# Thirteen more down products formed from fp32r parts, low parts divided anew between VectorE and GpSimd, and all steps of the iterations placed anew

## Chip, core and metric

The kernel runs on one core of one Trainium2 chip. The metric is the device time of one execution in microseconds. TensorE multiplies matrices, VectorE (DVE in the rows), ScalarE (ACT) and GpSimd (POOL) work on elements, SyncE (SP) issues most transfers; each runs its own queue in order and meets the others by semaphores.

## The reference

Eight sequences of 512 tokens with 128 channels pass four residual blocks, each behind a layer norm:

```python
x = x + attention(layernorm(x))      # causal, one head of 128
x = x + moe(layernorm(x))            # router, 32 experts, top 4, swiglu(128 -> 64 -> 128), and a shared swiglu(128 -> 128 -> 128)
x = x + time_and_channel_mix(layernorm(x))   # two norms, token shift, recurrence over 512 tokens; relu^2 MLP 128 -> 512 -> 128
x = x + moe(layernorm(x))            # the same experts again
def swiglu(x, w1, w2, w3): return silu(x @ w1) * (x @ w3) @ w2
```

Everything is float32. The expert block is computed for all tokens by all experts, each hidden value weighted by its token's router weight, which is zero for experts not chosen.

## The kernel before

**Iterations and units.** The expert block of one sequence and one layer is an iteration `g`, 0 to 15 (0 to 7 the first layer, 8 to 15 the second). An iteration has 17 units: 16 pairs of experts (2 x 64 hidden values, 128 partitions) and the shared expert as unit 16. A unit `p` is: gate product `pa` (L1039, L1040, L1043), linear product `pb` (the same lines), `m_th` = silu or tanh of pa on ScalarE (L732, L734), `m_v` = m_th x pb on VectorE (L1468, or L1449 and L1471 after a tanh), `m_h` = m_v x router weight `m_wb` on GpSimd (L587), and the down product `py`, which sums over the units.

**Two forms of the down product.** The up products are all formed from parts: a value is split in a high part, rounded to fp32r, and a low part, the rest; high x high, low x high and high x low are three fp32r matmuls. The down product of a unit is either *native*, one fp32 matmul of m_h that the hardware runs as two passes (L1067), or formed from parts: ScalarE makes the high part `m_hh` (L921), VectorE or GpSimd the low part `m_hl` = m_h - m_hh (L416, `split_low`), then three fp32r matmuls (L1072 to L1074). The table `NATIVE` says which units of an iteration are native, `LOW_ON_POOL` whose low part is made by GpSimd, `LOW_LATE` which low parts stand behind VectorE's m_v of their slot instead of ahead of it, `TANH` which gates go by tanh: there VectorE computes (tanh + 1) x pa first (L1449), one VectorE step more, and no silu. The parts have `HALVES` = 3 buffers, m_h has `HIDDEN` = 5.

**The order.** Nothing is scheduled while it runs. Each engine's function `iteration` loops over slots, three for each unit; a unit's own steps have fixed slots, and each other step (attention of a coming sequence `att_step`, router of the next iteration `pro_step`, recurrence `time_begin` and `time_finish`, channel mix `channel_step`, and adding the result `add_out`) has a slot in a tuple written in the code, one number per sequence. So a number moves a step ahead of or behind units in its engine's queue. TensorE's matmuls of unit p wait for m_th and m_v of unit p - 2; its down product runs `LAG` = 4 units behind.

**Names used below.** `a_p`, `a_pT` (L1780): the two blends of the channel mix; `f_xl` (L1747): a low part of it; `t_ri` (L1785): a quarter of a reciprocal; `r_sel` (L1618), `r_ws` (L604), `r_w` (L1628): the router's selection, weights before and after the limit; L1231 and L1235: the matmuls that count the chosen tokens; `x_sb` (L669): GpSimd's addition to the residual.

Of the kernel before, what the change touches and what calls it, by code (L numbers as in the profile page):

```python
# [101 lines left out]
    (0, 2, 6, 7, 10, 14),
    (0, 1, 6, 8, 11, 13, 15),
    (1, 2, 3, 7, 9, 10, 12, 13, 14, 15),
    (0, 2, 7, 12),
# [60 lines left out]
def hybrid_kernel(nc, x_in, att_mats, mats, key_in, vecs, w_gate, w1_in, w3_in, w2_in, x_out):  # L166
    with ExitStack() as ctx:
# [377 lines left out]
        def _(pool):  # L545
# [48 lines left out]
            def pro_step(q, slot):
                if slot == (20, 10, 6, 7, 4, 4, 7, 11, 5, 1, 7, 7, 9, 4, 6, 0)[q]:
                    rsqrt(r_rs[:, :], r_ve[:, :], "r_vedone", q + 1, "r_rstd")
                if slot == (30, 32, 25, 30, 28, 32, 24, 35, 34, 31, 22, 37, 30, 37, 30, 22)[q]:
# [1304 lines left out]
```

## Time and profile before

| | us |
|---|---|
| median of three runs | 793.85 |
| lowest, highest | 793.61, 794.05 |
| span of the profiled execution | 791.7 |
| TensorE busy | 785.1 |
| VectorE, ScalarE, GpSimd busy | 645.9, 567.9, 625.3 |

The span runs from the first to the last instruction; some time before and behind it belongs to a run. The profile gives instructions with start and duration. Starts are measured; the ends of matmuls are modelled, so distances between starts tell what a matmul takes from the queue.

### The profile page before, as it was taken

What the parts mean: (1) busy time and instruction counts of PE and PEld (TensorE: products, weight loads), DVE (VectorE), ACT (ScalarE), POOL (GpSimd) and SP (SyncE); (2) the same over time, 40 slices, a digit from 0 to 9 for tenths busy, and PEclk for the clock granted to TensorE, in tenths of its full rate; (3) what the DMA queues carried; (4) which work ended last, traced back from release to release, by engine and by line L of the source; (5) the groups of instructions that cost most, each with busy time, mean ns of one, the idle gap of its engine ahead of it and who ended that gap; (6) DMA issues with size and microseconds to landing.
All of it is one profiled execution on the core that took longest, in us unless ns stands there. A gap on an engine that the chain in (4) does not pass through costs nothing.

```text
span 791.7 us, 12780 instructions
## 1 busy us (share of the span) xinstructions
PE 785.1 (99%) x3817; PEld 596.4 (75%) x3817; DVE 645.9 (82%) x1539; ACT 567.9 (72%) x1055; POOL 625.3 (79%) x491
## 2 busy tenths in 40 slices
PE   8999999999999999999999999999999999999998
PEld 5777778676776777768778777887778767788786
DVE  6875577997997989998988869988689889767686
ACT  5677787868768778689765867668685775677553
POOL 6687779849767797769987888998797877876985
PEclk9999999999999999999999999999999999999999
DMA  9353334243144342462425444253444424425552
GB/s 326 95 123 82 87 92 113 66 102 92 42 113 113 73 105 54 110 133 58 120 60 134 104 93 107 65 143 79 110 113 95 90 68 110 111 59 115 124 127 74
DMA packets 49332, 80.73 MB, mean 102 GB/s; under 512 B 3280, under 2 KB 14544, under 8 KB 48880
## 3 DMA queue, kind: packets, MB, share of 16 engines
q1 hardware_dynamic: 48976, 79.72, 42.1%
q8 instruction: 31, 0.51, 0.3%
q14 instruction: 37, 0.30, 0.1%
q10 hardware_dynamic: 288, 0.20, 0.1%
HBM read 75.19 MB, written 4.72 MB: 101 GB/s over the span
## 4 chain that ended last, share of the span: by engine, by line
PE 51%; POOL 2%; issue 2%; DVE 1%; ACT 0%; DVEq 0%; POOLq 0%; ACTq 0%
PE pa L1039 5%; PE pb L1039 4%; PE py L1067 4%; PE pa L1043 4%; PE pb L1043 4%; PE pa L1040 4%; PE pb L1040 4%; PE pu L1326 4%; PE py L1072 3%; PE py L1074 3%; PE py L1073 3%; POOL m_h L587 1%; PE pq L1283 1%; PE pu L1310 1%; PE pv L1334 1%
## 5 line engine op out<-in xcount | busy, mean ns | idle before, releaser
L587 POOL TENSOR_TENSOR m_h<-m_v,m_wb 128x512 f32<-128x512 f32 x254 | 364.3, 1444 | 98.7 <-DVE m_v L1468 42.9
L732 ACT ACTIVATE m_th<-pa 128x512 f32<-128x512 f32 x220 | 130.6, 594 | 102.0 <-PE pa L1043 97.7
L1468 DVE TENSOR_TENSOR m_v<-m_th,pb 128x512 f32<-128x512 f32 x205 | 138.6, 679 | 23.9 <-ACT m_th L732 15.5
L1039 PE MATMUL pa<-m_xh,w1h 128*128 128x512 f32 x272 | 137.2, 504 | 0.3 <-DVE m_v L1471 0.2
L416 DVE TENSOR_TENSOR m_hl<-m_h,m_hh 128x512 fp32r<-128x512 f32 x120 | 111.4, 929 | 24.8 <-ACT m_hh L921 24.1
L921 ACT ACTIVATE m_hh<-m_h 128x512 fp32r<-128x512 f32 x184 | 115.2, 626 | 13.8 <-POOL m_h L587 13.1
L1039 PE MATMUL pb<-m_xh,w3h 128*128 128x512 f32 x272 | 115.4, 424 | 0.0
L1043 PE MATMUL pa<-m_xl,w1h 128*128 128x512 f32 x272 | 107.3, 394 | 0.3 <-POOL m_xl L608 0.3
L1043 PE MATMUL pb<-m_xl,w3h 128*128 128x512 f32 x272 | 107.1, 394 | 0.0
L1040 PE MATMUL pa<-m_xh,w1l 128*128 128x512 f32 x272 | 106.6, 392 | 0.0
L1040 PE MATMUL pb<-m_xh,w3l 128*128 128x512 f32 x272 | 106.5, 391 | 0.0
L416 POOL TENSOR_TENSOR m_hl<-m_h,m_hh 128x512 fp32r<-128x512 f32 x64 | 86.1, 1345 | 12.6 <-ACT m_hh L921 12.1
L1072 PE MATMUL py<-m_hh,w2h 128*128 128x512 f32 x183 | 77.2, 422 | 0.0
L1074 PE MATMUL py<-m_hl,w2h 128*128 128x512 f32 x183 | 72.0, 394 | 0.0
L1073 PE MATMUL py<-m_hh,w2l 128*128 128x512 f32 x183 | 71.6, 392 | 0.0
L1039 PEld LDWEIGHTS pa<-m_xh,w1h 128*128 128x128 f32 x272 | 51.5, 189 | 25.5 <-issue 14.4
L1040 PEld LDWEIGHTS pa<-m_xh,w1l 128*128 128x128 f32 x272 | 51.5, 189 | 20.6 <-issue 14.6
L1039 PEld LDWEIGHTS pb<-m_xh,w3h 128*128 128x128 f32 x272 | 51.3, 189 | 14.0 <-issue 3.9
L1043 PEld LDWEIGHTS pa<-m_xl,w1h 128*128 128x128 f32 x272 | 51.1, 188 | 12.2 <-POOL m_xl L608 0.7
L1043 PEld LDWEIGHTS pb<-m_xl,w3h 128*128 128x128 f32 x272 | 51.1, 188 | 11.6
L1040 PEld LDWEIGHTS pb<-m_xh,w3l 128*128 128x128 f32 x272 | 51.4, 189 | 10.8 <-issue 1.9
L1449 DVE SCALAR_TENSOR_TENSOR m_th<-m_th,pa 128x512 f32<-128x512 f32 x52 | 35.2, 677 | 15.9 <-ACT m_th L734 15.8
(318 smaller groups left out, 1653.8 us busy)
## 6 DMA issues: line engine op xcount, KB each, us to landing
m_wb<-w_scratch SPq DMA_DIRECT2D x126, 512.0 KB, 6.5
x_sb<-in_x SPq DMA_DIRECT2D x8, 256.0 KB, 7.2
m_wb<-in_w SPq DMA_DIRECT2D x2, 1024.0 KB, 6.8
x_out<-x_sb SPq DMA_DIRECT2D x7, 256.0 KB, 6.6
u_scratch<-t_u SPq DMA_DIRECT2D x6, 256.0 KB, 2.6
t_u<-u_scratch SPq DMA_DIRECT2D x6, 256.0 KB, 2.7
f_kk<-in_w SPq DMA_DIRECT2D x1, 1024.0 KB, 9.7
w_scratch<-r_wT SPq DMA_DIRECT2D x16, 64.0 KB, 1.5
```

The source lines that it names most:

```text
L416: eng.tensor_tensor(m_hl[:, at, :], hidden(g, p), m_hh[:, at, :].bitcast(F32), ALU.subtract)\
L587: pool.tensor_tensor(hidden(g, p), gated(g, p), m_wb[:, p % (GRING * GP), :], ALU.mult).then_inc(sig["m_h"], 1)
L732: ins = act.activation(m_th[:, p % 2, :], pa[p % 2][:, :], ACT.Silu)
L921: act.activation(m_hh[:, halves_at(g, p), :], hidden(g, p), ACT.Copy).then_inc(sig["m_hh"], 1)
L1039: pe.matmul(ps[:, :], high[:, p, :], xh, start=True, stop=False)
L1040: pe.matmul(ps[:, :], low[:, p, :], xh, start=False, stop=False)
L1043: return pe.matmul(ps[:, :], high[:, p, :], xl, start=False, stop=True)
L1072: pe.matmul(py[:, :], w2h[:, p, :], hh, start=(p == 0), stop=False)
L1073: pe.matmul(py[:, :], w2l[:, p, :], hh, start=False, stop=False)
L1074: pe.matmul(py[:, :], w2h[:, p, :], hl, start=False, stop=(p == last_down(g))).then_inc(sig["m_y"], 1)
L1449: dve.scalar_tensor_tensor(out=m_th[:, r, :], in0=m_th[:, r, :], scalar=1.0, in1=pa[r][:, :], op0=ALU.add, op1=ALU.mult).then_inc(sig["m_u ...
L1468: dve.tensor_tensor(gated(g, p), m_th[:, r, :], pb[r][:, :], ALU.mult).then_inc(sig["m_v"], 1)
```

## The change

Thirteen units leave `NATIVE`: one in iterations 0, 1, 2, 4, 8 and 11, two in 3 and 6, three (1, 9, 11) in 7. Of their low parts VectorE makes eleven and GpSimd two; of the others, unit 14 of iterations 7 and 13, unit 16 of 14 and unit 3 of 15 go from GpSimd to VectorE, and unit 16 of iteration 2 the other way, so that VectorE makes 134 in place of 120 and GpSimd 63 in place of 64. 55 gates go by tanh in place of 52. Nearly all tuples of slots have new numbers, on all four engines; no step is added or dropped otherwise, and buffers, semaphores and fillers stay.

```diff
 NATIVE = (
-    (3, 9),
-    (11,),
-    (2, 3, 5, 6, 9, 10, 11, 12, 13),
-    (1, 2, 3, 4, 5, 7, 9, 10, 11, 12, 13, 14, 15),
-    (3, 5, 6, 7, 9, 10, 11, 13, 16),
+    (3,),
+    (),
+    (3, 5, 6, 9, 10, 11, 12, 13),
+    (1, 2, 3, 5, 7, 9, 10, 11, 12, 14, 15),
+    (3, 5, 6, 7, 10, 11, 13, 16),
     (1, 2, 7, 9, 10, 11, 12, 13),
-    (1, 3, 5, 7, 9, 15),
-    (1, 5, 7, 9, 11),
-    (1, 3, 5, 7, 9, 11, 16),
+    (3, 7, 9, 15),
+    (5, 7),
+    (1, 3, 5, 7, 11, 16),
...
 LOW_ON_POOL = (
...
-    (1, 2, 4, 8, 11, 12, 14),
-    (1, 3, 6, 8, 9, 10),
+    (2, 4, 8, 12),
+    (1, 3, 6, 8, 10),
...
             def channel_step(m, slot):
-                if slot == (40, 36, 38, 43, 41, 38, 44, 23)[m]:
+                if slot == (43, 45, 47, 46, 34, 37, 44, 22)[m]:
                     kept(pool, m)
                     pool.tensor_tensor(wide(chunk(m)), wide(chunk(m)), wide(t_u2[:, :, :]), ALU.add)\
                         .then_inc(sig["f_x"], 1)
```

**TensorE, iteration 7, around the linear product pb of unit 14.** Before, from the channel mix's product pu to the count of chosen tokens (L1231):

```order
L1310 MATMUL pu<-mt,a_pT 128x128 x4
L1039 MATMUL pb<-m_xh,w3h 128x512
L1040 MATMUL pb<-m_xh,w3l 128x512
L1043 MATMUL pb<-m_xl,w3h 128x512
L1334 MATMUL pv<-f_xh,key_h 128x512
L1335 MATMUL pv<-f_xh,key_l 128x512
L1336 MATMUL pv<-f_xl,key_h 128x512
L1231 MATMUL pq<-r_sel,tri_b 128x128
```

And now:

```order
L1310 MATMUL pu<-mt,a_pT 128x128 x4
L1231 MATMUL pq<-r_sel,tri_b 128x128
L1235 MATMUL pq<-r_sel,ones_b 128x128
L1235 MATMUL pq<-r_sel,ones_b 128x96
L1235 MATMUL pq<-r_sel,ones_b 128x64
L1235 MATMUL pq<-r_sel,ones_b 128x32
L1039 MATMUL pb<-m_xh,w3h 128x512
L1040 MATMUL pb<-m_xh,w3l 128x512
L1043 MATMUL pb<-m_xl,w3h 128x512
```

The count, which waits for r_sel, moved ahead of pb of unit 14; five matmuls stood between before.

**VectorE, the same place.** Before, from m_v of unit 11 to m_v of unit 13:

```order
L1468 TENSOR_TENSOR m_v<-m_th,pb 128x512
L1785 RECIPROCAL t_ri<-t_xr 128x128
L1780 SCALAR_TENSOR_TENSOR a_p<-a_g,vec,a_xT 128x512
L416 TENSOR_TENSOR m_hl<-m_h,m_hh 128x512
L1747 TENSOR_TENSOR f_xl<-a_p,f_xh 128x512
L1780 SCALAR_TENSOR_TENSOR a_pT<-a_g,vec,a_xT 128x512
L1468 TENSOR_TENSOR m_v<-m_th,pb 128x512
L1618 TENSOR_SCALAR r_sel<-r_rep 128x128
L1716 TENSOR_TENSOR t_n<-t_n,t_xv 128x512
L1468 TENSOR_TENSOR m_v<-m_th,pb 128x512
```

And now:

```order
L1468 TENSOR_TENSOR m_v<-m_th,pb 128x512
L416 TENSOR_TENSOR m_hl<-m_h,m_hh 128x512
L1785 RECIPROCAL t_ri<-t_xr 128x128
L1780 SCALAR_TENSOR_TENSOR a_p<-a_g,vec,a_xT 128x512
L1780 SCALAR_TENSOR_TENSOR a_pT<-a_g,vec,a_xT 128x512
L1747 TENSOR_TENSOR f_xl<-a_p,f_xh 128x512
L416 TENSOR_TENSOR m_hl<-m_h,m_hh 128x512
L1468 TENSOR_TENSOR m_v<-m_th,pb 128x512
L1618 TENSOR_SCALAR r_sel<-r_rep 128x128
L1468 TENSOR_TENSOR m_v<-m_th,pb 128x512
L416 TENSOR_TENSOR m_hl<-m_h,m_hh 128x512
L1716 TENSOR_TENSOR t_n<-t_n,t_xv 128x512
```

A second low part (that of unit 9) stands between m_v of unit 11 and of unit 12, and one more behind m_v of unit 13.

**GpSimd, the same place.** Before, from the channel mix's difference a_g on:

```order
L675 TENSOR_TENSOR a_g<-a_xT 128x512
L587 TENSOR_TENSOR m_h<-m_v,m_wb 128x512
L599 TENSOR_TENSOR r_p<-r_ex,r_ri 128x128
L587 TENSOR_TENSOR m_h<-m_v,m_wb 128x512
L669 TENSOR_TENSOR x_sb<-x_sb,t_u 128x512
L604 TENSOR_TENSOR r_ws<-r_sel,r_p 128x128
```

And now:

```order
L675 TENSOR_TENSOR a_g<-a_xT 128x512
L587 TENSOR_TENSOR m_h<-m_v,m_wb 128x512 x3
L599 TENSOR_TENSOR r_p<-r_ex,r_ri 128x128
L604 TENSOR_TENSOR r_ws<-r_sel,r_p 128x128
L587 TENSOR_TENSOR m_h<-m_v,m_wb 128x512
L416 TENSOR_TENSOR m_hl<-m_h,m_hh 128x512
```

The addition to x_sb left its place ahead of r_ws; it stands some units later.

## Rows read from the trace of the kernel before

**Rows 1.** The page: span, busy time of each engine, granted TensorE clock in forty slices.

```profile
span 791.7 us, 12780 instructions
PE 785.1 (99%) x3817; PEld 596.4 (75%) x3817; DVE 645.9 (82%) x1539; ACT 567.9 (72%) x1055; POOL 625.3 (79%) x491
PEclk9999999999999999999999999999999999999999
```

**Rows 2.** Busy time by stretches: start:end, length, each engine, clock, transfers.

```profile
0.00:24.20 24.20, 21.96 (x121) 14.21 (x121) 15.40 (x67) 13.65 (x34) 13.47 (x26) 1.00 0.89 291
24.20:373.70 349.50, 349.07 (x1695) 260.09 (x1694) 286.70 (x738) 269.17 (x504) 269.55 (x210) 1.00 0.39 91
373.70:419.50 45.80, 45.80 (x229) 35.86 (x228) 41.22 (x84) 31.84 (x57) 40.38 (x31) 1.00 0.45 106
419.50:748.80 329.30, 328.51 (x1606) 254.78 (x1605) 270.97 (x609) 231.83 (x425) 269.87 (x205) 1.00 0.43 100
748.80:791.70 42.90, 39.80 (x177) 31.47 (x176) 31.57 (x43) 21.38 (x38) 32.04 (x23) 1.00 0.40 99
```

**Rows 3.** Timeline of TensorE in iteration 7: start, duration, instruction.

```profile
402.60 0.39 PE L1072 MATMUL py<-m_hh,w2h 128*128 128x512 f32 x1
...
403.29 0.39 PE L1039 MATMUL pa<-m_xh,w1h 128*128 128x512 f32 x1
...
404.66 1.02 PE L1067 MATMUL py<-m_h,w2f 128*128 128x512 f32 x2
405.12 0.79 PE L1039 MATMUL pa<-m_xh,w1h 128*128 128x512 f32 x1
405.75 0.39 PE L1040 MATMUL pa<-m_xh,w1l 128*128 128x512 f32 x1
```

**Rows 4.** Groups and lines: count, busy and mean, or minimum/median/maximum ns.

```profile
L921 ACT ACTIVATE m_hh<-m_h 128x512 fp32r<-128x512 f32 x184 | 115.2, 626 | 13.8 <-POOL m_h L587 13.1
L416 DVE TENSOR_TENSOR m_hl<-m_h,m_hh 128x512 fp32r<-128x512 f32 x120 | 111.4, 929 | 24.8 <-ACT m_hh L921 24.1
L416 DVE TENSOR_TENSOR m_hl<-m_h,m_hh x120: 671/693/1792, 41.0 to 786.3; 128x512 fp32r<-128x512 f32 x120
L416 DVE TENSOR_TENSOR m_hl<-m_h,m_hh 128x512 fp32r<-128x512 f32 x6 | 6.9, 1150 | 0.0
L1449 DVE SCALAR_TENSOR_TENSOR m_th<-m_th,pa 128x512 f32<-128x512 f32 x52 | 35.2, 677 | 15.9 <-ACT m_th L734 15.8
L587 POOL TENSOR_TENSOR m_h<-m_v,m_wb x254: 1260/1300/2208, 38.9 to 784.4; 128x512 f32<-128x512 f32 x127
```

**Rows 5.** Timeline of VectorE in iteration 7, and TensorE's pb of unit 14.

```profile
401.30 0.68 DVE L1468 TENSOR_TENSOR m_v<-m_th,pb 128x512 f32<-128x512 f32 x1
...
402.75 1.68 DVE L1780 SCALAR_TENSOR_TENSOR a_p<-a_g,vec,a_xT 128x512 f32<-128x512 f32 x1
404.36 0.88 DVE L416 TENSOR_TENSOR m_hl<-m_h,m_hh 128x512 fp32r<-128x512 f32 x1
...
405.77 0.74 DVE L1780 SCALAR_TENSOR_TENSOR a_pT<-a_g,vec,a_xT 128x512 f32<-128x512 f32 x1
406.43 0.68 DVE L1468 TENSOR_TENSOR m_v<-m_th,pb 128x512 f32<-128x512 f32 x1
407.03 0.22 DVE L1618 TENSOR_SCALAR r_sel<-r_rep 128x128 bf16<-128x128 f32 x1
...
407.72 0.48 PE L1039 MATMUL pb<-m_xh,w3h 128*128 128x512 f32 x1
```

**Rows 6.** Timeline of GpSimd in the same stretch.

```profile
402.59 1.29 POOL L587 TENSOR_TENSOR m_h<-m_v,m_wb 128x512 f32<-128x512 f32 x1
...
407.24 1.76 POOL L587 TENSOR_TENSOR m_h<-m_v,m_wb 128x512 f32<-128x512 f32 x1 [2.55 <-issue]
408.97 1.29 POOL L669 TENSOR_TENSOR x_sb<-x_sb,t_u 128x512 f32<-128x512 f32 x1
```

**Rows 7.** Timeline of the end: the last instruction of TensorE.

```profile
788.21 0.38 PE L1394 MATMUL pu<-ident,m_y 128*128 128x128 f32 x2
```

More of the change, by code:

```diff
@@ L65 @@
 LOW_ON_POOL = (
-    (0, 2, 3, 7, 8, 9, 11, 12, 13, 14),
+    (0, 2, 3, 7, 8, 11, 12, 13, 14),
     (3, 4, 7, 10, 11, 13, 14, 15),
-    (2, 3, 6, 9, 10, 13, 14),
-    (3, 4, 6, 9, 10, 13),
-    (1, 7, 9, 14, 15),
+    (3, 6, 9, 10, 13, 14, 16),
+    (3, 6, 9, 10, 13),
+    (1, 7, 14, 15),
     (4, 5, 10, 12, 13, 14),
     (7, 11, 12),
-    (1, 2, 4, 8, 11, 12, 14),
-    (1, 3, 6, 8, 9, 10),
+    (2, 4, 8, 12),
+    (1, 3, 6, 8, 10),
     (0, 1, 3, 4, 6, 7, 11, 12, 14, 15),
@@ L78 @@
     (2, 5, 9, 12, 14, 15),
-    (4, 6, 7, 8, 10, 11, 14),
-    (12, 13, 14, 16),
-    (3, 9, 12, 16),
+    (4, 6, 7, 8, 10, 11),
+    (12, 13, 14),
+    (9, 12, 16),
 )
@@ L90 @@
 LOW_LATE = (
-    (0, 1, 3, 6, 7, 10, 13, 14, 15, 16),
+    (0, 1, 3, 6, 7, 9, 10, 13, 14, 15, 16),
     (0, 2, 4, 7, 9, 10, 16),
-    (1, 4, 7, 10, 12),
-    (1, 7, 11, 15),
-    (2, 4, 10, 12, 13),
+    (1, 2, 4, 7, 10, 12, 15),
+    (1, 4, 7, 11, 15),
+    (2, 4, 9, 10, 12, 13),
     (1, 8, 11, 16),
-    (2, 6, 8, 13, 15, 16),
-    (0, 1, 2, 3, 5, 6, 7, 8, 11, 12, 16),
-    (1, 7, 8, 12, 16),
+    (1, 2, 6, 8, 13, 15, 16),
+    (0, 1, 2, 3, 5, 6, 7, 8, 9, 11, 12, 14, 16),
+    (1, 7, 8, 9, 12, 16),
     (2, 10, 13, 15),
     (1, 2, 3, 5, 7, 10, 11),
[L102 to L105, printed above, removed]
+    (0, 2, 6, 7, 10, 14, 16),
+    (0, 1, 6, 11, 13, 15),
+    (1, 2, 3, 7, 9, 10, 12, 13, 15),
+    (0, 2, 6, 7, 12),
     (0, 1, 2, 5, 6, 7, 9, 10, 14, 16),
@@ L109 @@
 TANH = (
-    (0, 1, 6, 8, 11, 14),
+    (0, 1, 6, 8, 11, 14, 15),
     (15,),
@@ L114 @@
     (4, 6, 12, 13),
-    (12, 13),
+    (8, 12, 13),
     (12, 13, 15),
@@ L120 @@
     (2, 9, 13, 15),
-    (3, 9, 13, 15),
-    (1, 5, 11, 12, 16),
+    (3, 5, 9, 13, 15),
+    (5, 11, 12, 16),
     (3, 5, 8),
-    (),
-    (1, 2, 3, 4, 7, 9, 12),
+    (4, 9),
+    (1, 3, 4, 7, 9, 12),
 )
@@ L617, in weights_step @@
                     low_quarter(0, w3l, w3, w3h, 2)
-                if slot == (9,)[0]:
+                if slot == (6,)[0]:
                     low_quarter(1, w1l, w1, w1h, 1)
-                if slot == (24,)[0]:
+                if slot == (21,)[0]:
                     low_quarter(1, w3l, w3, w3h, 2)
-                if slot == (14,)[0]:
+                if slot == (8,)[0]:
                     low_quarter(2, w1l, w1, w1h, 1)
-                if slot == (23,)[0]:
+                if slot == (35,)[0]:
                     low_quarter(2, w3l, w3, w3h, 2)
-                if slot == (14,)[0]:
+                if slot == (11,)[0]:
                     low_quarter(3, w1l, w1, w1h, 1)
-                if slot == (35,)[0]:
+                if slot == (30,)[0]:
                     low_quarter(3, w3l, w3, w3h, 2)
-                if slot == (35,)[0]:
+                if slot == (37,)[0]:
                     low_quarter(0, w2l, w2_stage, w2h, 3)
-                if slot == (36,)[0]:
+                if slot == (39,)[0]:
                     low_quarter(1, w2l, w2_stage, w2h, 3)
@@ L1249, in spread_step @@
             def spread_step(slot):
-                if slot == (34,)[0]:
+                if slot == (38,)[0]:
                     pe.wait_ge(sig["r_wT"], 1)
@@ L1565, in pro_step @@
             def pro_step(q, slot, cmix):
-                if slot == (16,)[0] and q == 0:
+                if slot == (19,)[0] and q == 0:
                     dve.wait_ge(sig["a_add"], 2)
@@ L1787, in first_step @@
             def first_step(slot):
-                if slot == (27,)[0]:
+                if slot == (29,)[0]:
                     open_gate(0, 0)
                     gate(0, 0)
-                if slot == (35,)[0]:
+                if slot == (34,)[0]:
                     open_gate(0, 1)
                     gate(0, 1)
-                if slot == (35,)[0]:
+                if slot == (32,)[0]:
                     weigh(0)
-                if slot == (39,)[0]:
+                if slot == (38,)[0]:
                     weigh(1)
```

284 lines of the change are left out of this document (142 added, 142 removed), and 2 rows, old and new, of the table NATIVE.

## The prediction

> **What bounds the kernel now.** I read the busy line of the page first, then the busy time by stretches, then the instructions around one loaded place, and last the end. TensorE is busy 785.1 of 791.7 us, and its granted clock is full in all forty slices [rows 1]. So TensorE sets the time, and the question for every edit is whether it takes TensorE time away or makes TensorE wait. The stretches say where TensorE idles at all: 2.24 us before 24.2 us, 0.43 us in the first seven iterations, nothing in iteration 7, 0.79 us in iterations 8 to 14, and 3.1 us in the last one [rows 2]. That last part stands behind the last transpose (788.21 + 0.38), where VectorE adds and the output is stored [rows 7]; nothing in the change touches it. A busy TensorE can still hide short waits, since the ends of matmuls are modelled, but what idles openly inside the iterations is 0.43 + 0.79 = 1.2 us in all. Waits that the change removes can therefore bring little.
>
> The other engines have room, though not the same in every iteration. Over the span VectorE is busy 645.9, ScalarE 567.9, GpSimd 625.3 us [rows 1]. In iteration 7 VectorE is busy 41.22 of 45.80 us [rows 2], the tightest of those that the change loads most. Why this does not stop TensorE: TensorE works two units behind. At one place of iteration 7 VectorE's product m_v of unit 12 ends at 406.43 + 0.68 = 407.11, and the linear matmul that waits for it, pb of unit 14, starts at 407.72 [rows 5]: 0.6 us to spare, after five other steps had stood before it.
>
> **The change, part by part.**
>
> *Thirteen down products formed from parts.* Each removes one fp32 product (two passes, py<-m_h) and adds three fp32r products (py<-m_hh, m_hh, m_hl). The busy column misleads here, because a pass reads 590 ns and a fp32r product 390 ns while they overlap; the distance of starts counts. Three fp32r products start at 402.60 and the next unit's matmul at 403.29: 0.69 us. The fp32 product starts at 404.66; the record of the matmul after it begins early, inside the second pass, so I take the start of the one after that, 405.75, less one spacing of 0.23: 405.52, thus 0.86 us [rows 3]. Saved: 0.86 - 0.69 = 0.17 us a unit, 13 x 0.17 = 2.2 us, all on TensorE, which sets the end. No new matmuls elsewhere and the same fillers: TensorE's other work stays.
>
> *What they cost.* ScalarE makes 13 more high parts, 13 x 0.626 = 8.1 us on an engine that is busy 72% [rows 1, 4]: hidden. The low parts: VectorE makes 134 in place of 120, GpSimd 63 in place of 64. On VectorE one takes 929 ns in the mean, 671 at least, 693 in the median and 1792 at most [rows 4]. So 14 more cost 14 x 0.69 = 9.7 us if nothing blocks them, 13.0 us at the mean, 25.1 us at the worst row. Three more gates by tanh add three first steps, 3 x 0.68 = 2.0 us [rows 4]. VectorE goes from 646 to 658 to 661 us (83%); ACT_TABLE_LOADs stay at 62. Taken over the whole span this is hidden; by iterations it is not sure. Iteration 7 gets four of the fourteen (units 1, 9 and 11 newly formed, unit 14 taken from GpSimd). The six it has now take 6.9 us, 1150 ns each [rows 4]; at that price VectorE needs 41.2 + 4 x 1.15 = 45.8 us in an iteration that shrinks to 45.8 - 3 x 0.17 = 45.3. At 0.69 each it needs 44.0. What hides a low step is then gone to within -0.5 to +1.3 us, and VectorE also has waits of its own for TensorE that do not close up.
>
> *The steps placed anew.* The stretch of 929 over 693 ns is a low step that waits beside GpSimd: the scaling a_p starts at 402.75, takes 1.68 us where its sister a_pT takes 0.74, and GpSimd's m_h starts at 402.59 and runs 1.29 us [rows 5, 6]: VectorE stood until it ended. GpSimd pays too: m_h at 407.24 takes 1.76 against a median of 1.30 [rows 4, 6]. The Trainium skill ("SBUF — State Buffer", section Who interferes with whom) states it as a lock: a VectorE instruction with two SBUF inputs contends with a GpSimd instruction that reads SBUF, and the later one waits for the whole of the other. It speaks against this change, since each added low part has two SBUF inputs; the rows agree with it, and by it the fourteen could cost between 9.7 us and the 25.1 us of the worst row. Better placement gives VectorE and GpSimd time, and TensorE none unless it waits for them. I cost it at nothing, within bounds of -1.2 us (all open waits of the iterations go) and +1.6 us (somewhat more than as many come again).
>
> *One place by hand.* In iteration 7, from the start of m_v of unit 11 (401.30) to the end of r_sel (407.03 + 0.22 = 407.25), VectorE needs 5.95 us, with 0.94 us of blocking on a_p and 0.19 on the low step. After the change a second low step stands in this row (+0.69) and, if nothing blocks, 1.13 go: 5.5 us; if one step is blocked as a_p is now, 6.45 us. TensorE then asks for r_sel directly before pb of unit 14, so at 407.72 - 401.30 = 6.42 us behind the same point, 6.25 with the product of unit 9 shortened. So 0.7 us to spare or a wait of 0.2 us [rows 3, 5]. To the good, GpSimd's x_sb addition of 1.29 us (408.97) leaves its place before r_ws [rows 6]. I take 0.4 us of new waits in all, two such places, between 0 and 1.6.
>
> *The opening.* TensorE idles openly there for 2.24 us [rows 2]. On VectorE the shift a_sh and the conversion of w3 move behind one x_sb update, and on ScalarE r_ex moves ahead of two exponentials; the sum of the work before the router is the same. I cost this at nothing, within +-0.5 us.
>
> **Sum.** The profiled span is 791.7 us, the median of the three runs 793.85: 2.1 us lie around the span and stay. 791.7 - 2.2 + 0.4 = 789.9 us of span, so 792.0 us. A measurement of this kernel can tell about 0.2%, 1.6 us, from no change; the forecast of 1.8 us lies just past it.
>
> **The rivals.**
> 1. *Placement also removes waits.* With all of the product's saving and two thirds of the 1.2 us of open waits: 793.85 - 2.2 - 0.8 = 790.8 us. For it: nothing on TensorE stands against it. Against it: the waits of now are small and scattered, and VectorE gets 12 us more work.
> 2. *The saving is eaten by VectorE.* The price is the upper bound of new waits, 1.6 us, and somewhat more in iterations 3, 6 and 7, which take two or three new units each: 793.2 us, at most no change. For it: 0.6 us to spare at the place above. It is also the case that the new places do not avoid the blocking, so the change would not do what it says.
> 3. *Slower.* Iteration 7 becomes VectorE's. If its four new low steps are blocked as the worst row (1.79 us each), VectorE needs 41.2 + 7.2 = 48.4 us against 45.3: 3.1 us of wait, since pa and pb of each unit wait for m_v of two units before, and the backlog is carried into iteration 8. With one more iteration of this kind (6 or 3, half as much) it is 793.85 - 2.2 + 3.1 + 1.5 = 796.2 us. It begins to cost where the four steps take more than (45.3 - 41.2) / 4 = 1.0 us in the mean, and makes the kernel slower past 1.6 us in the mean. For it: 1.15 us is the mean there now. Against it: median 0.69, and a blocked step also ends blocks for the next.
>
> Less likely still is a long wait of ScalarE for the ring of three high and low parts, which now is passed by more units: iterations 13 and 14 hold 15 formed units of 17 already, as iteration 7 will, and lie in the stretch that loses 0.79 us in all [rows 2].
>
> **How the numbers follow.** Forecast (791.2 to 792.8): 0.45. Rival 1 (790.0 to 791.2): 0.18. Rival 2 (792.8 to 795.0): 0.21. Rival 3 (above 795): 0.16. The range 790.2 to 795.4 leaves out a little at the bottom and most of rival 3. Faster by over 0.2% means below 792.26: rival 1 and two thirds of the forecast, 0.50. Slower by over 0.2% means above 795.44: 0.15, nearly all of rival 3. The rest, 0.35, is the same.
>
> **What would show it.** Matmuls py<-m_hh 196 in place of 183, two-pass py<-m_h 26 fewer; TensorE busy lower by about 2 us and iteration 7 shorter by 0.5. Low parts on VectorE x134: a mean near 0.7 says that the placing works, 0.93 that it does nothing. TensorE's open idle in the stretches stays at 6.5 us in all. The forecast is wrong if starts of pa or pb wait for m_v in iterations 6 to 8, if VectorE shows no idle in iteration 7, or if the opening ends later than 24.2 us.

## The result and the profile after

| | median, us | lowest, highest | ratio to before, 95% interval |
|---|---|---|---|
| kernel before | 793.92 | 793.61, 794.05 | |
| changed kernel | 803.69 | 803.41, 804.33 | 1.0126 [1.0112, 1.0141] |

The change makes the kernel 9.8 us slower. The forecast was 792.0 us with a range up to 795.4: it has the wrong sign and its range does not hold the time.

The head of the page of the changed kernel, answering to [rows 1]:

```profile
span 802.0 us, 12854 instructions
PE 788.1 (98%) x3830; PEld 595.7 (74%) x3830; DVE 659.1 (82%) x1556; ACT 574.8 (72%) x1068; POOL 631.6 (79%) x490
PEclk9999999999999999999999999999999999999999
```

The clock is full, as before. VectorE's 659.1 us is what the prediction had (658 to 661). ScalarE has 6.9 us more than before, against the 8.1 reckoned for its high parts. GpSimd, for which the prediction gave no figure and which makes one low part less, is busier by 6.3 us. TensorE is not less busy by 2.2 us but busier by 3.0. Busy time by stretches, answering to [rows 2]; the third is iteration 7:

```profile
0.00:24.10 24.10, 21.39 (x121) 14.03 (x121) 15.40 (x67) 13.62 (x33) 13.48 (x26) 1.00 0.89 292
24.10:376.30 352.20, 350.48 (x1703) 259.99 (x1702) 297.55 (x745) 275.27 (x513) 279.06 (x214) 1.00 0.39 90
376.30:422.60 46.30, 45.65 (x232) 36.39 (x231) 41.46 (x87) 32.00 (x59) 40.82 (x29) 1.00 0.39 91
422.60:759.30 336.70, 331.07 (x1606) 253.81 (x1605) 273.25 (x615) 232.87 (x427) 270.06 (x204) 1.00 0.43 97
759.30:802.00 42.70, 39.54 (x177) 31.48 (x175) 31.44 (x44) 21.05 (x37) 28.23 (x20) 1.00 0.49 117
```

The opening and the last iteration with the end are no longer (24.1 and 42.7 us). The iterations between are 10.6 us longer: 2.7 in the first seven, 0.5 in iteration 7, 7.4 in the seven behind it, 3.1 of these in iteration 10 alone (from 49.7 to 52.8 us). TensorE's open idle is now 802.0 - 788.1 = 13.9 us, against 791.7 - 785.1 = 6.6.

Groups and lines, answering to [rows 3] and [rows 4] (count, busy, mean ns; idle before and what ended most of it):

```profile
L1072 PE MATMUL py<-m_hh,w2h 128*128 128x512 f32 x196 | 82.4, 420 | 0.4 <-POOL m_hl L416 0.4
L921 ACT ACTIVATE m_hh<-m_h 128x512 fp32r<-128x512 f32 x197 | 123.3, 626 | 21.1 <-POOL m_h L587 20.5
L416 DVE TENSOR_TENSOR m_hl<-m_h,m_hh 128x512 fp32r<-128x512 f32 x134 | 119.6, 894 | 22.0 <-ACT m_hh L921 21.4
L587 POOL TENSOR_TENSOR m_h<-m_v,m_wb 128x512 f32<-128x512 f32 x254 | 368.4, 1459 | 106.5 <-DMA m_wb<-w_scratch 42.7
```

The counts are those of the change. A low part on VectorE takes 894 ns in the mean: it was 929, and 0.7 us was the mark for "the placing works". GpSimd now waits 42.7 us in all for the transfer that brings the router weights, m_wb; in the same group of the kernel before, most of the idle time was for VectorE:

```profile
L587 POOL TENSOR_TENSOR m_h<-m_v,m_wb 128x512 f32<-128x512 f32 x254 | 364.3, 1444 | 98.7 <-DVE m_v L1468 42.9
```

For the transfer it waited 12.3 us there, in 5 places. What TensorE waits for, after (total us, times, longest):

```profile
PE pa L1039 <- DVE m_v L1471: 2.3, 4, 0.9
...
PE pq L1231 <- ACT t_r L855: 1.5, 2, 0.8
...
```

Before, that view has nothing above 0.3 us but the 1.6 us of the opening:

```profile
PE pq L977 <- POOL minus_half L551: 1.6, 1, 1.6
PE pv L1218 <- ACT m_xh L808: 0.3, 1, 0.3
```

There is no one new bottleneck: beside the same 1.6 us of the opening the view lists many waits of 0.2 to 0.9 us, for VectorE, ScalarE and GpSimd alike.

**How large the waits are in all.** The saving of the products is real. TensorE in iteration 7 of the changed kernel:

```profile
402.87 1.02 PE L1067 MATMUL py<-m_h,w2f 128*128 128x512 f32 x2
...
403.96 0.39 PE L1040 MATMUL pa<-m_xh,w1l 128*128 128x512 f32 x1
...
405.10 0.39 PE L1072 MATMUL py<-m_hh,w2h 128*128 128x512 f32 x1
...
405.79 0.39 PE L1039 MATMUL pa<-m_xh,w1h 128*128 128x512 f32 x1
```

403.96 - 402.87 - 0.23 = 0.86 us for the two passes, 405.79 - 405.10 = 0.69 us for the three fp32r products, as in [rows 3]. Wherever in this kernel a gate product pa stands right behind the down product, the distances are the same: 0.86 us in the median of 26 native products, 0.69 in that of 158 from parts. Without any new wait a kernel with the 13 parts would have a span of 791.7 - 2.2 = 789.5 us. The changed kernel has 802.0: 12.5 us of new waits. Of these 7.3 show as idle (13.9 - 6.6); the other 5.2 are counted as busy (788.1 - 785.1 + 2.2). Below, "new waits" is always the span less 789.5 (kernels with the parts) or less 791.7 (without them).

### The profile page after: what moved, and what is told of

It is laid out like the page before. It is cut to its first block and busy times, and to the rows that moved or that the text cites. A ratio compares the mean times of both kernels' runs of the same rounds, so it can differ in the third digit from the quotient of the medians.

```text
span 802.0 us, 12854 instructions
## 1 busy us (share of the span) xinstructions
PE 788.1 (98%) x3830; PEld 595.7 (74%) x3830; DVE 659.1 (82%) x1556; ACT 574.8 (72%) x1068; POOL 631.6 (79%) x490
## 5 line engine op out<-in xcount | busy, mean ns | idle before, releaser
L587 POOL TENSOR_TENSOR m_h<-m_v,m_wb 128x512 f32<-128x512 f32 x254 | 368.4, 1459 | 106.5 <-DMA m_wb<-w_scratch 42.7
L732 ACT ACTIVATE m_th<-pa 128x512 f32<-128x512 f32 x217 | 128.8, 594 | 102.5 <-PE pa L1043 95.6
L921 ACT ACTIVATE m_hh<-m_h 128x512 fp32r<-128x512 f32 x197 | 123.3, 626 | 21.1 <-POOL m_h L587 20.5
L416 DVE TENSOR_TENSOR m_hl<-m_h,m_hh 128x512 fp32r<-128x512 f32 x134 | 119.6, 894 | 22.0 <-ACT m_hh L921 21.4
L1039 PE MATMUL pa<-m_xh,w1h 128*128 128x512 f32 x272 | 132.2, 486 | 3.2 <-DVE m_v L1471 2.3
L1039 PE MATMUL pb<-m_xh,w3h 128*128 128x512 f32 x272 | 117.4, 432 | 0.7 <-DVE m_v L1468 0.5
L1072 PE MATMUL py<-m_hh,w2h 128*128 128x512 f32 x196 | 82.4, 420 | 0.4 <-POOL m_hl L416 0.4
L1074 PE MATMUL py<-m_hl,w2h 128*128 128x512 f32 x196 | 77.1, 393 | 0.0
L1073 PE MATMUL py<-m_hh,w2l 128*128 128x512 f32 x196 | 76.7, 391 | 0.0
L1072 PEld LDWEIGHTS py<-m_hh,w2h 128*128 128x128 f32 x196 | 36.9, 188 | 12.0 <-issue 3.3
```

The costliest lines, as they stand in the source:

```text
L416: eng.tensor_tensor(m_hl[:, at, :], hidden(g, p), m_hh[:, at, :].bitcast(F32), ALU.subtract)\
L587: pool.tensor_tensor(hidden(g, p), gated(g, p), m_wb[:, p % (GRING * GP), :], ALU.mult).then_inc(sig["m_h"], 1)
L732: ins = act.activation(m_th[:, p % 2, :], pa[p % 2][:, :], ACT.Silu)
L921: act.activation(m_hh[:, halves_at(g, p), :], hidden(g, p), ACT.Copy).then_inc(sig["m_hh"], 1)
L1039: pe.matmul(ps[:, :], high[:, p, :], xh, start=True, stop=False)
L1072: pe.matmul(py[:, :], w2h[:, p, :], hh, start=(p == 0), stop=False)
```

## The experiments

All times are medians; the kernel before took 792.7 to 793.9 us beside them, so times of runs that did not stand beside each other compare to about 1 us, and better by their ratios. Spans and waits are those of the one profiled execution.

**1. The parts alone, the places alone.** e1 is the kernel before with the `NATIVE` of the changed kernel and the low parts of just these 13 units as there; e2 is the kernel before with all slots of the changed kernel and its own four tables.

```diff
 # e1_parts_only: only the tables
 NATIVE = (
-    (3, 9),
-    (11,),
+    (3,),
+    (),
...
 # e2_places_only: only the slots
-                if slot == (40, 36, 38, 43, 41, 38, 44, 23)[m]:
+                if slot == (43, 45, 47, 46, 34, 37, 44, 22)[m]:
...
```

> The kernel before with only the thirteen units of the change formed from parts: NATIVE as after, the low parts of these units on the engine and in the half slot that the change gives them, every other step where it stood before. Theory P (the new places of the steps cost the time, the parts save it): TensorE saves 2.2 us and waits little more, 791.5 to 793.0 us. Theory V (VectorE's added low parts cost it): eleven more low parts of 0.9 us stand in unchanged queues and the worst of it shows here, 799 us or more.

> The slots of all steps as after, the four tables (NATIVE, LOW_ON_POOL, LOW_LATE, TANH) as before. Theory P: without the parts' saving of 2.2 us but with the waits, 803 to 806 us. Theory V: 793 to 795 us.

Measured: e1 803.6 us, ratio 1.0129 [1.0114, 1.0145], span 801.8; e2 803.7 us, 1.0134 [1.0119, 1.0150], span 802.0. Each half alone costs what both cost together: 12.3 us of new waits for the parts at the old places, 10.3 for the new places without the parts, 12.5 for both. So the new places do hold the parts better (they bring 12.3 us of waits at the old places and 2.2 more at the new, just what their products save), but are themselves 10 us worse. Two causes had to be looked for.

**2. Why the parts cost 12 us: take the added work away, piece by piece.** In e1, e6 makes the 13 added low parts for 64 of 512 tokens, e9 the high parts too; e14 makes no added low part at all (a memset of one column, 59 ns on VectorE and 99 on GpSimd, keeps its waits and its signal), e15 is e14 with short high parts.

```diff
 # e6, e9 (low parts)
+            n = 64 if (g, p) in ADDED else S
-            eng.tensor_tensor(m_hl[:, at, :], hidden(g, p), m_hh[:, at, :].bitcast(F32), ALU.subtract)\
+            eng.tensor_tensor(m_hl[:, at, 0:n], hidden(g, p)[:, 0:n], m_hh[:, at, 0:n].bitcast(F32), ALU.subtract)\
 # e9, e15 (high parts)
-                act.activation(m_hh[:, halves_at(g, p), :], hidden(g, p), ACT.Copy).then_inc(sig["m_hh"], 1)
+                n = 64 if (g, p) in ADDED else S
+                act.activation(m_hh[:, halves_at(g, p), 0:n], hidden(g, p)[:, 0:n], ACT.Copy).then_inc(sig["m_hh"], 1)
 # e14, e15 (low parts)
+            if (g, p) in ADDED:
+                eng.memset(m_hl[:, at, 0:1].bitcast(F32), 0.0).then_inc(sig[signal], 1)
+                return
```

> e1_parts_only, with the low parts of the thirteen added units computed for 64 of their 512 tokens only (the rest of their buffers keeps what stood there), so that each takes some 0.2 us in place of 0.7 to 1.8 of VectorE or GpSimd; ScalarE's high parts and TensorE's three products stay. Theory V (in the old places the time of the low step delays m_v and what stands behind it): the waits of 12 us go and the saving of 2.2 us remains, 791.5 to 794.5 us. If ScalarE's added high parts or the ring of three buffers is what TensorE waits for: 800 us or more.

> The kernel e6_low_short with, besides the low parts, the high parts of the 13 added units too made for 64 of 512 tokens only (that part of the output is not computed). TensorE still has 773.2 us of own work, against 775.4 in the kernel before; every step stands in its queue with its waits, only the 13 added steps of ScalarE are about 0.5 us shorter each. e6_low_short took 798.5 us, with 7.3 us more TensorE waits than the kernel before. Theory: the rest of these waits is ScalarE's added time, 0.63 us each, which makes m_th, the copies for the router and the norm late for TensorE. Then most of it goes and the time is 791.5 to 793.5 us. Rival: it is the place in the queue and not the time: ScalarE stands at an added high part until GpSimd's m_h is there, and what is behind it starts late however short the step is. Then the time stays at 797 to 799 us. In between, both count, in that share.

> The kernel e1_parts_only in which the 13 added low parts are not made: in place of each stands a memset of one column with the same wait and signal, so that what these products add is not computed; their fp32r matmuls and high parts stay. In e6_low_short the 11 steps on VectorE for 64 tokens still took 643 ns in the mean (one 1.30 us beside GpSimd's m_h), against 218 at least and 937 for the whole ones, so that experiment took away only a third of VectorE's added time. Theory: the waits come from the time that the low steps hold VectorE and GpSimd, standing beside each other's instructions included. From e1_parts_only to e6_low_short the time fell by 5.1 us for about 5.2 us less work on both; the remaining 7.7 us would bring all of the rest, down to 791.5 to 794 us, about the kernel before less the 2.2 us of the products. Rival: what costs is that ScalarE stands at an added high part for GpSimd's m_h, and that a product now needs two steps more before it, m_hh and m_hl, however short: then it stays at 796.5 to 799 us.

> The same as e14_no_low, and the 13 added high parts for 64 of 512 tokens only: nearly all added work of the three engines is gone, and only the waits at the added places are left. By the first theory 791 to 792.5 us, at most 1 us under e14_no_low; by the rival still 796 us or more.

| | median | ratio to before, interval | span | new waits | new waits by the median |
|---|---|---|---|---|---|
| e1, all work | 803.6 | 1.0129 [1.0114, 1.0145] | 801.8 | 12.3 | 12.3 |
| e6, low short | 798.5 | 1.0068 [1.0053, 1.0083] | 796.7 | 7.2 | 7.2 |
| e9, low and high short | 798.6 | 1.0068 [1.0051, 1.0085] | 795.0 | 5.5 | 7.3 |
| e14, no low | 795.0 | 1.0020 [1.0011, 1.0030] | 793.8 | 4.3 | 3.7 |
| e15, no low, high short | 793.4 | 1.0002 [0.9993, 1.0011] | 791.6 | 2.1 | 2.1 |

The last column takes the median less 1.8 us (what lies around the span) in place of the profiled span. It matters for e9, whose profiled execution was the fastest of its four (796.7): short high parts brought nothing on top of short low parts.

The low steps are 8.6 of the 10.3 us that e1 lies above before (803.6 - 795.0), the high steps 1.6 (795.0 - 793.4). 2.1 us of waits remain with hardly any work left, and take back the product's whole saving. So of 2.2 us saved nothing is left even where the added work is nearly free.

Where they stand can be read from e15: no down product of TensorE shows a wait there. Its longest wait that the kernel before does not have is for a copy of ScalarE, r_p, in the stretch of iteration 3, which takes 1.2 us more than before. ScalarE, then TensorE, in e15:

```profile
188.71 0.26 ACT L927 ACTIVATE m_hh<-m_h 128x64 fp32r<-128x64 f32 x1 [1.88 <-POOL m_h L592]
...
194.66 0.33 PE L1230 MATMUL pq<-ident,r_p 128*128 128x128 f32 x1 [0.80 <-ACT r_p L817]
```

And the same place of ScalarE before:

```profile
186.75 1.64 ACT L904 ACTIVATE a_xn<-x_sb,a_sh,a_q 128x128 f32<-128x128 f32 x4
```

An added high part of 0.26 us makes ScalarE stand 1.88 us for GpSimd's m_h. The step behind it, a_xn, started at 186.75 before and starts at 188.87 now, and r_p behind that at 194.34 in place of 192.68. So it is the place of the high part in ScalarE's queue, not its length. Of the remaining 0.9 us 0.4 stand in iteration 11, where TensorE waits 0.5 us for another copy of ScalarE, t_k; the rest is not followed.

From e6 and e9 alone one would read that ScalarE's time is no cause and only its place in the queue is. e14 and e15 show that both are. The groups of e6 show why short low steps were no clean test; the first row is VectorE's, and under it stand GpSimd and VectorE in iteration 8 at one of the added units:

```profile
L418 DVE TENSOR_TENSOR m_hl<-m_h,m_hh 128x64 fp32r<-128x64 f32 x11 | 7.1, 643 | 1.8 <-ACT m_hh L923 1.8
```

```profile
455.72 1.29 POOL L589 TENSOR_TENSOR m_h<-m_v,m_wb 128x512 f32<-128x512 f32 x1
455.79 1.30 DVE L418 TENSOR_TENSOR m_hl<-m_h,m_hh 128x64 fp32r<-128x64 f32 x1
```

A step for an eighth of the tokens, 218 ns at the least, takes 643 in the mean and here 1.30 us: it ends at 457.09, 0.08 us behind GpSimd's m_h beside it. Against the 937 ns of the group in e1 shortening had removed only a third of VectorE's added time. e14, which puts a step without SBUF inputs in its place, was the test.

How one such step becomes a wait of TensorE shows in e1, iteration 8 (all engines, in order of start):

```profile
459.72 1.29 POOL L587 TENSOR_TENSOR m_h<-m_v,m_wb 128x512 f32<-128x512 f32 x1
459.77 1.79 DVE L416 TENSOR_TENSOR m_hl<-m_h,m_hh 128x512 fp32r<-128x512 f32 x1
...
464.38 1.80 DVE L1671 SCALAR_TENSOR_TENSOR t_ea<-t_pp,decay 128x512 f32<-128x512 f32 x1
...
466.21 1.06 ACT L859 ACTIVATE t_ea<-t_ea 128x1024 f32<-128x1024 f32 x1 [2.34 <-DVE t_ea L1671]
...
467.18 0.61 ACT L921 ACTIVATE m_hh<-m_h 128x512 fp32r<-128x512 f32 x1
...
467.87 1.26 POOL L416 TENSOR_TENSOR m_hl<-m_h,m_hh 128x512 fp32r<-128x512 f32 x1 [2.24 <-ACT m_hh L921]
...
469.28 0.47 PE L1072 MATMUL py<-m_hh,w2h 128*128 128x512 f32 x1 [1.23 <-POOL m_hl L416]
```

The added low part (459.77) is blocked beside m_h; VectorE's step t_ea of the recurrence comes late and is blocked in its turn; ScalarE stands 2.34 us for t_ea, and behind that exponential stands the high part of another unit; GpSimd stands 2.24 us for it, and TensorE 1.23 us for the low part. In the kernel before, no low step stands at this place; t_ea takes 0.90 us there, and the same down product, formed from parts before too, does not wait. So here the price is paid through VectorE, ScalarE and GpSimd by steps behind the edit, not by the new step's own product.

The parts have three buffers, and a fourth might seem a remedy. The traces give it nothing to remove: neither in e1 nor in the changed kernel does a high part wait for TensorE to give a buffer back; the only waits listed for m_hh (19.9 and 20.5 us) are for GpSimd's m_h.

**3. Why the new places cost 10 us: the late router.** In the changed kernel TensorE's transpose of the weights (L1246, slot in L1239) and ScalarE's copy r_wT (L823, slot in L816) stand later for many iterations. e4 makes only this change to the kernel before; e3 and e5 undo it in the changed kernel, e3 for the weights of all iterations but 8 and 14, e5 for those of iterations 3 to 7, 9, 12, 13 and 15. In some of them both also move VectorE's r_w and TensorE's count to their earlier slots.

```diff
 # e4_router_end_late (kernel before)
-                if slot == (37, 43, 41, 43, 43, 43, 42, 43, 43, 43, 44, 44, 44, 47, 42, 39)[q]:
+                if slot == (38, 43, 41, 44, 46, 44, 44, 45, 48, 46, 44, 44, 45, 52, 44, 43)[q]:
...
-                if slot == (31, 44, 41, 44, 42, 44, 42, 44, 45, 47, 45, 46, 44, 47, 46, 39)[q]:
+                if slot == (31, 44, 41, 45, 45, 44, 42, 44, 48, 47, 45, 47, 45, 48, 47, 45)[q]:
```

> The kernel after, with the last steps of the router (the count's matmuls L1226 ff, VectorE's r_w, the transpose of r_w, ScalarE's copy r_wT that the transfer of the weights waits for) at the earlier of their two slots, before's or after's, in all iterations but 8 and 14. Theory R (the weights of the next iteration land late, GpSimd waits for them 42.7 us in place of 12.3, and TensorE with it): 796 to 800 us, and GpSimd's wait for the landing near 15 us. If the landing is not what TensorE waits for: 802 to 805 us.

> The kernel before, with only the transpose of r_w on TensorE and the copy r_wT on ScalarE at the later of their two slots, before's or after's. Theory R: GpSimd's wait for the landing rises from 12 to about 40 us and the kernel takes 797 to 801 us. If the landing does not matter: 793.5 to 795 us.

> The kernel after, with the last steps of the router at the earlier of their two slots only for the weights of iterations 3 to 7, 9, 12, 13 and 15, where the earlier count of L1226 stood behind nothing it had to wait for. Theory R (late weights are most of what the new places cost): TensorE's waits in iterations 3, 4, 6, 9, 13 and 14 fall by 5 us as they did in the run before, nothing new comes, 797.5 to 800 us. If the new places lose as much elsewhere once these waits are gone: 801.5 us or more.

Measured: e4 802.3 us, ratio 1.0118 [1.0094, 1.0143]: two tuples of slots alone cost nearly as much as the whole change. In iteration 8 of e4 one can follow it:

```profile
417.02 0.27 ACT L823 ACTIVATE r_wT<-pq 128x128 f32<-128x128 f32 x1
...
417.31 0.33 SPq L506 DMA_DIRECT2D w_scratch<-r_wT  x1
...
419.77 2.56 SPq L522 DMA_DIRECT2D m_wb<-w_scratch  x4
...
427.65 1.29 POOL L587 TENSOR_TENSOR m_h<-m_v,m_wb 128x512 f32<-128x512 f32 x1 [6.02 <-DMA m_wb<-w_scratch]
...
430.35 1.64 POOL L572 TENSOR_TENSOR t_q<-t_ve,minus_half 128x8 f32<-128x8 f32 x1
...
432.02 0.23 DVE L1435 TENSOR_REDUCE t_nm<-t_q 128x4 f32<-128x8 f32 x2 [1.68 <-POOL t_q L572]
432.16 0.68 DVE L1468 TENSOR_TENSOR m_v<-m_th,pb 128x512 f32<-128x512 f32 x1
...
432.90 0.51 PE L1039 MATMUL pb<-m_xh,w3h 128*128 128x512 f32 x1 [1.64 <-DVE m_v L1468]
```

From the end of r_wT (417.29) to the first m_h of the iteration it is 10.4 us, 6.02 of them a wait of GpSimd. In the kernel before r_wT starts 5.1 us earlier and the first m_h 4.4 us earlier, at 423.22. Behind the late m_h stands GpSimd's t_q for a norm, VectorE stands 1.68 us for it, m_v stands behind that, and TensorE pays 1.64 us at 432.90. GpSimd's total wait for the transfer is 47.9 us in e4, 42.7 in the changed kernel, 12.3 before.

Undoing most of it gives back little: e5 took 801.4 us, ratio 1.0104 [1.0089, 1.0119], 2.3 us under the changed kernel (1.7 by the ratios), though GpSimd's wait fell to 21.4 us. e3 became slower, 807.0 us, 1.0170 [1.0153, 1.0187]: in iterations 1 and 10 it also moves the count of chosen tokens (L1231) ahead to where r_sel and t_r are not ready,

```profile
PE pq L1231 <- ACT t_r L855: 2.8, 2, 2.1
PE pq L1231 <- DVE r_sel L1618: 2.7, 1, 2.7
```

So lateness of the router is a cause that is enough by itself, but not the one cause of the loss: with most of it gone, e5 still lies 8.3 us above the kernel before. It is no clean removal, since e5 leaves the weights of iterations 8, 11 and 14 late, and in e4 iterations 8 and 14 lose most (2.8 and 2.9 us, from the first gate product of one iteration to that of the next). But in e5 these three are only 1.1, 0.0 and 0.3 us longer than before, so what was left late explains little of the 8.3.

**4. Is the loss local?** e7 is the changed kernel with all steps of iteration 10 as before, e11 with those of 4, 9, 10 and 13, e17 is e7 with the early router of e5; e8 is the kernel before with iterations 12 and 15 as in the changed one.

```diff
 # e7_iteration10_back, one of its lines (m = 4 belongs to iteration 10)
-                if slot == (43, 45, 47, 46, 34, 37, 44, 22)[m]:
+                if slot == (43, 45, 47, 46, 41, 37, 44, 22)[m]:
```

> The kernel after, with all steps of iteration 10 (which has no added unit) as before. If each iteration loses on its own account: TensorE's wait of 3.4 us in iteration 10 falls to about 0.4, and the kernel takes 800.2 to 801.5 us. If a lateness is only handed on to the next iteration: 803 us or more.

> The kernel before, with all steps and tables of iterations 12 and 15 as after, the only two in which TensorE waits less in the profile of after (0.30 against 0.54 us and 0.14 against 0.38). If losses and gains are local: 793.0 to 794.0 us, at or a little below before. If they depend on what the neighbours hand over: 795 us or more.

> The changed kernel with all steps and tables of iterations 4, 9, 10 and 13 as in the kernel before, and everything else changed. With iteration 10 alone put back it took 799.7 us; there the starts of TensorE left waits of 0.52 us in iteration 4, 0.97 in iteration 9 and 2.19 in iteration 13, against 0.20, 0.03 and 0.00 in the kernel before. Theory: the loss is local, each iteration whose orders were changed loses on its own account. Then these three give back 0.3 + 0.9 + 2.2 us less 0.2 us for the product of iteration 4 formed from parts: 796.5 us. Rival: a seam between an old and a new order costs as much as it gives, since the steps for coming iterations are spread over several; then it stays at 799 us or more.

> The changed kernel with iteration 10 as before (alone: 799.7 us, 4.0 less than the changed kernel) and the end of the router at the earlier slots for the weights of iterations 3 to 7, 9, 12, 13 and 15 (alone: 801.4 us, 2.3 less). Theory: the losses are separate and add up: 803.7 - 4.0 - 2.3 = 797.4 us. Rival: they are partly the same time, because a TensorE that waits less at one place comes too early at the next, where the other engines are no faster: then it stays at 799 us or more.

Measured: e7 799.7 us, 1.0083 [1.0068, 1.0098], so 4.0 us come back (3.4 by the ratios) for an iteration that had grown by 3.1; e8 793.4 us, 1.0007 [0.9997, 1.0017], no change. e11 799.8 us, 1.0078 [1.0063, 1.0093]: three more iterations put back bring nothing more by the time (the theory said 796.5), and only the rival was right. e17 798.2 us, 1.0064 [1.0047, 1.0082]; the sum said 797.4 and the rival 799 or more, and the interval (797.0 to 799.7) holds both. So a large local fault can be cut out by itself; that the rest is no sum over iterations rests on e11 alone.

**5. Inside iteration 10.** All four tables are unchanged in iteration 10, so its loss is placing alone. The first of its two places in the changed kernel, VectorE, GpSimd and TensorE:

```profile
546.77 0.29 DVE L1591 TENSOR_REDUCE r_mx<-pv 128x4 f32<-128x128 f32 x1 [0.52 <-PE pv L1224]
...
547.17 1.26 POOL L608 TENSOR_TENSOR m_xl<-t_v,m_xh 128x512 fp32r<-128x512 f32 x1
...
547.30 1.68 DVE L1780 SCALAR_TENSOR_TENSOR a_p<-a_g,vec,a_xT 128x512 f32<-128x512 f32 x1
...
548.91 0.68 DVE L1471 SCALAR_TENSOR_TENSOR m_v<-m_th,pb 128x512 f32<-128x512 f32 x1
...
549.64 0.50 PE L1039 MATMUL pa<-m_xh,w1h 128*128 128x512 f32 x1 [0.64 <-DVE m_v L1471]
```

The same place before:

```profile
541.34 1.52 DVE L1780 SCALAR_TENSOR_TENSOR a_p<-a_g,vec,a_xT 128x512 f32<-128x512 f32 x1
...
542.79 0.67 DVE L1471 SCALAR_TENSOR_TENSOR m_v<-m_th,pb 128x512 f32<-128x512 f32 x1
```

a_p is blocked as in [rows 5], but it was before too (1.52 us), with the same m_v right behind it, which was just in time: it ended at 543.46 and pa started at 543.55. VectorE's order is the same there. New are 0.52 us that its r_mx stands for the transpose of the logits (L1224), which TensorE made ahead of the gate product before and makes behind it now, and 0.16 us more of blocking. At the second, ScalarE makes t_eb, t_r and t_ea in this order and TensorE stands for t_r:

```profile
561.58 1.28 ACT L863 ACT_TABLE_LOAD   x1 [1.90 <-DVE t_eb L1675]
...
563.85 0.58 ACT L855 ACTIVATE t_r<-pq 128x512 f32<-128x512 f32 x1
...
564.57 0.22 PE L1231 MATMUL pq<-r_sel,tri_b 128*128 128x128 bf16 x1 [0.78 <-ACT t_r L855]
...
567.33 0.50 PE L1039 MATMUL pa<-m_xh,w1h 128*128 128x512 f32 x1 [0.65 <-ACT m_th L732]
```

Two kernels change one number each there; e13 is the changed kernel itself on the chip of e12.

```diff
 # e12_one_step_back: GpSimd's x_sb (L669), iteration 10, from beside t_eb to five steps later
-                if slot == (43, 45, 47, 46, 34, 37, 44, 22)[m]:
+                if slot == (43, 45, 47, 46, 41, 37, 44, 22)[m]:
 # e16_t_r_first: ScalarE's t_r ahead of t_eb
-                if slot == (37, 40, 36, 38, 41, 38, 40, 37)[m]:
+                if slot == (37, 40, 36, 38, 41, 38, 39, 37)[m]:
```

> The changed kernel with one number as in the kernel before: GpSimd's addition to x_sb (L669) in iteration 10 stands at slot 41 again in place of 34. In the changed kernel it started at 559.68, right beside VectorE's t_eb (L1675), which took 1.40 us there against 0.98 in the kernel before; ScalarE stood 1.90 us for that t_eb, its t_r ended at 564.43, and TensorE's count (L1231) started at 564.57 after a wait of 0.9 us; ScalarE's next m_th was late too, and pa at 567.33 waited 0.8 us. Theory: the loss of an iteration is a chain of such places, each one step on GpSimd that VectorE and then ScalarE and TensorE wait behind. Then t_eb takes about 0.7 to 1.0 us, both waits shrink by 0.4 to 0.7 each, and the time is 0.8 to 1.4 us below that of the changed kernel on the same chip. Rival: GpSimd is so full there that its next step, m_h of 1.3 us, takes the place of the addition and blocks t_eb just the same. Then the waits stay and the time is within 0.4 us of the changed kernel's.

> The changed kernel itself, without an edit, beside e12_one_step_back on the same chip, so that about 1 us can be told: 803.4 to 804.3 us by both theories, and 10 us above the kernel before.

> The changed kernel with one number: in iteration 10 ScalarE makes t_r (L855) ahead of the exponential t_eb (L863) and its table load in place of behind it (the kernel before has both exponentials ahead of t_r, but started them 2.3 us earlier within the iteration). TensorE's count (L1231) waited 0.9 us for t_r there. Theory: this is an order at fault and the wait goes with it: the count no longer waits and the time falls by 0.5 to 1.3 us, to about 802.5 us. Rival: ScalarE's group of t_r, two exponentials and two table loads has the same length, and pa at 567 waits for the m_th behind it; what the count no longer waits is waited for there: within 0.5 us of the changed kernel.

Measured: e13 802.6 us (802.43 to 802.91), e12 803.3 (801.92 to 804.65), e16 803.2, 1.0121 [1.0104, 1.0138]: no gain by either number. In e12 m_h (559.25, 1.27 us) has taken the place of x_sb,

```profile
559.68 1.39 DVE L1675 SCALAR_TENSOR_TENSOR t_eb<-t_k,vec,t_h 128x512 f32<-128x512 f32 x1
```

and t_eb still takes 1.39 us. In e16 the count no longer waits, but the group on ScalarE is as long as in the changed kernel (5.2 us from t_r to m_th, against 5.1 from the table load to m_th), and pa waits 1.16 us in place of 0.65:

```profile
566.06 0.50 PE L1039 MATMUL pa<-m_xh,w1h 128*128 128x512 f32 x1 [1.16 <-ACT m_th L732]
```

Both rivals were right. A wait at this place is the end of a queue's lateness, and moving one step hands it on.

**Left open.** Of the 9.8 us that the changed kernel loses, iteration 10 and the late router together account for about 5 (803.7 to 798.2, e17; 4.9 by the ratios). The rest is spread: in e17's profile, the slowest of its four executions, iterations 0, 5, 7, 8, 11, 14 and 15 are each 0.5 to 0.9 us longer than before and iteration 13 1.8, and no run names the causes one by one. No kernel here points below the kernel before; what would be safest, one unit in iteration 0, would save 0.17 us, which no measurement could tell.

## Why the prediction was wrong

*TensorE sets the time, and every edit must be asked whether it makes TensorE wait:* right, and answered too lightly.

*The products save 2.2 us:* right, 0.86 and 0.69 us again. The prediction expected TensorE's busy time to fall by as much. It rose by 3.0, since 5.2 us of the new waits are counted as busy; the sign that the prediction named could not have shown the saving.

*New waits of 0.4 us, between 0 and 1.6:* the term that failed. With the parts alone it is 12.3 us. Its bounds came from one place reckoned and from how little TensorE waited before. That TensorE waited for nothing was read as room; where it was looked at, steps came just in time (in iteration 10 m_v ended 0.1 us before pa started). The prediction named 0.6 us to spare at pb of unit 14 and let 9.7 to 13 us of new work on VectorE meet such margins at 14 places. e14 and e1 put the price of the low steps at 8.6 us, for 11 steps of 0.94 us and 2 on GpSimd of 1.3: about two thirds of their own length reached TensorE. With what they block they keep VectorE busy 13.8 us longer (658.6 against 644.8) and GpSimd 5.7, and against these 19.5 us it is somewhat under a half.

*High parts on ScalarE, 8.1 us at 72% busy, hidden:* wrong in part. Making them short takes 4.6 us from ScalarE and 1.6 from the time (e14 to e15). A share of the whole span says little of a queue in which a step stands behind others.

*The place of a high part in ScalarE's queue:* at nothing in the prediction. ScalarE stands there for GpSimd's m_h however short its own step is; 2.1 us of waits stay when both parts cost almost nothing (e15), as much as the products save, and 1.2 of them stand in iteration 3 behind one such place.

*The placing, at nothing, -1.2 to +1.6:* the second term that failed, with 10.3 us (e2). The prediction asked only what blocking the placing might remove. It did not ask which of the moved steps has somebody waiting far away. It did not follow r_wT to w_scratch, m_wb and m_h, where two tuples cost 9.0 us by the medians (e4, whose four times lie 4.4 us apart).

*Blocking of VectorE beside GpSimd:* the mechanism was right, the measure of it too. The prediction said that 0.93 us would mean that the placing does nothing; it is 0.89. The Trainium skill ("SBUF — State Buffer", section Who interferes with whom) calls the port pair that VectorE shares with GpSimd an exclusive lock, for which a VectorE instruction with two SBUF inputs contends with a GpSimd instruction that reads SBUF. The trace of e6 agrees: the short low step beside m_h takes 1.30 us and ends 0.08 us behind it.

*The place by hand, iteration 7:* r_sel ended 0.43 us before its matmul asked (410.37 + 0.22 = 410.59, asked at 411.02), inside the bounds of 0.7 to spare and 0.2 of wait. That was luck: from the start of m_v of unit 11 (403.88) VectorE took 6.71 us, not 5.5 to 6.45, and TensorE came late itself; 0.65 us earlier, at 410.37, it would have waited 0.2 us. The row was also read for the wrong waiter. The channel mix's f_xl stands in it ahead of r_sel, behind the low part of unit 9 and, in the new order, behind a_pT too:

```profile
404.42 1.74 DVE L416 TENSOR_TENSOR m_hl<-m_h,m_hh 128x512 fp32r<-128x512 f32 x1
...
408.56 0.69 DVE L1747 TENSOR_TENSOR f_xl<-a_p,f_xh 128x512 fp32r<-128x512 f32 x1
...
409.35 0.47 PE L1334 MATMUL pv<-f_xh,key_h 128*128 128x512 f32 x1 [0.65 <-issue]
```

The low step is blocked (1.74 us), f_xl ends at 409.25, and TensorE's pv, which by the code waits for it, starts 0.1 us behind it after a wait of 0.65. The view names no releaser; e2, with the same places and no parts, lists no such wait.

*Rival 3, iteration 7 becomes VectorE's:* right in sign, wrong in mechanism and place. VectorE is busy 41.46 of 46.30 us there, and iteration 7 grew by 0.5 only. No iteration had to become any engine's for the loss to come. *Opening and end:* as predicted.

## What to carry to other kernels

If the engine that sets the time hardly waits, its neighbours may not be idle beside it but just in time. Here added work on them cost a third to two thirds of its length, so price it at such a part and only then subtract what a margin at a named place covers. Ask too what a new step makes its queue stand for, even where the step itself is short. A reorder of a tuned static schedule is never an edit at nothing; follow each moved step to its last waiter, through transfers too, and expect that two good halves (parts, places) can each be worse than neither. An experiment that shortens a step must show in its own trace that the step became shorter.

## What the hardware showed that was not expected

A VectorE step with two inputs for 64 of 512 tokens took 1.30 us beside a GpSimd step of 1.29 us, and 218 ns at the least: there its length was set by the step beside it and not by its own work. From the end of r_wT to the first use of the weights it spread took 10.4 us (iteration 8 of e4), through two transfers, the last 6.02 of them with GpSimd idle. In e12 VectorE's r_sel, one input of 128 columns, took 0.21 us; at the same place of the changed kernel, beside GpSimd's m_h, it took 1.32.
